# Adapter stage: the up products in two halves, VectorE's scale behind the next statistics, ScalarE's cast of z behind the gelu

## What is computed

```
h = gelu(z @ W_down[role] + b_down[role])        # 512 -> 256
u = h @ W_up[role] + b_up[role]                  # 256 -> 512
y = z + u
out = (y - mean(y)) * rsqrt(var(y) + 1e-5) * gamma[role] + beta[role]   # over the 512 features
```

## Time and profile before

| | us |
|---|---|
| median of 3 runs | 2029.14 (2028.83 to 2029.5) |
| profiled execution | 2028.81 |
| its span | 2027.2 |
| TensorE busy in the span | 2003.1 (99%) |
| VectorE busy | 1384.4 (68%) |
| ScalarE busy | 961.0 (47%) |
| GpSimd busy | 71.6 (4%) |
| adapter, from the first to the last transposes of `hs` | 116.84 |
| in it: TensorE, VectorE, ScalarE, GpSimd busy | 114.08, 107.85, 86.20, 40.94 |

### The profile page before, as it was taken

One profiled execution on the slowest core, in us unless ns is written; L12 is line 12 of the kernel. 1 busy time (PEld: TensorE's weight loads), 2 busy tenths in 40 slices (PEclk: granted clock), 3 DMA queues, 4 the chain that ended last, 5 costly groups with the idle time before them and its releaser, 6 DMA issues.

```text
span 2027.2 us, 28055 instructions
## 1 busy us (share of the span) xinstructions
PE 2003.1 (99%) x9338; PEld 1667.6 (82%) x9338; DVE 1384.4 (68%) x2567; ACT 961.0 (47%) x2009; POOL 71.6 (4%) x157
## 2 busy tenths in 40 slices
PE   8999999999999999999999999999999999999997
PEld 7888888888888878888888888888888888888886
DVE  6786785556777686555786785554787686654897
ACT  4654453433654444334564453343474454433675
POOL 0000000000000000000000000000000000000133
PEclk9999999999999999999999999999999999999999
DMA  4011232214112132124211231223202133212754
GB/s 167 32 63 42 73 104 63 63 37 151 63 52 63 53 125 63 32 63 146 73 53 42 73 99 58 63 63 120 99 32 63 43 108 115 94 58 75 258 166 126
DMA packets 106541, 169.01 MB, mean 83 GB/s; under 512 B 11168, under 2 KB 70816, under 8 KB 102688
## 3 DMA queue, kind: packets, MB, share of 16 engines
q1 hardware_dynamic: 98544, 128.81, 20.5%
q0 software_dynamic: 7776, 38.28, 5.3%
q10 hardware_dynamic: 80, 0.13, 0.0%
HBM read 136.51 MB, written 30.67 MB: 82 GB/s over the span
## 4 chain that ended last, share of the span: by engine, by line
PE 91%; DVE 4%; SPq 2%; issue 2%; DMA 1%; ACT 0%; DVEq 0%; POOL 0%; ACTq 0%; POOLq 0%
PE y L1728 16%; PE y L1730 16%; PE y L1729 16%; PE x L1728 13%; PE x L1729 13%; PE x L1730 13%; SPq L462 1%; PE y L1817 1%; PE x L1842 1%; SPq L470 1%; DVE w_lo L1155 1%; DVE c_forms L1317 0%; DVE f L1221 0%; SPq L481 0%; PE y L1816 0%
## 5 line engine op out<-in xcount | busy, mean ns | idle before, releaser
L682 ACT CAST w_hi<-w_blocks 128x512 fp32r<-128x512 f32 (+1 forms) x464 | 231.2, 519 | 122.2 <-PE y L1730 84.5
L1155 DVE TENSOR_TENSOR w_lo<-w_blocks,w_hi 128x512 fp32r<-128x512 f32 (+1 forms) x464 | 249.5, 563 | 54.7 <-ACT w_hi L682 54.7
L1728 PE MATMUL x<-h_hi,w_hi 128*128 128x512 f32 x512 | 199.7, 390 | 0.0
L1728 PE MATMUL y<-h_hi,w_hi 128*128 128x512 f32 x512 | 199.5, 390 | 0.0
L1729 PE MATMUL x<-h_lo,w_hi 128*128 128x512 f32 x512 | 199.3, 389 | 0.0
L1730 PE MATMUL x<-h_hi,w_lo 128*128 128x512 f32 x512 | 199.3, 389 | 0.0
L1729 PE MATMUL y<-h_lo,w_hi 128*128 128x512 f32 x512 | 199.3, 389 | 0.0
L1730 PE MATMUL y<-h_hi,w_lo 128*128 128x512 f32 x512 | 199.3, 389 | 0.0
L1728 PE MATMUL y<-a_forms,w_hi 128*128 128x512 f32 x480 | 187.8, 391 | 1.2 <-DVE f L1258 1.2
L1729 PE MATMUL y<-a_forms,w_hi 128*128 128x512 f32 x480 | 186.9, 389 | 0.0
L1730 PE MATMUL y<-a_forms,w_lo 128*128 128x512 f32 x480 | 186.9, 389 | 0.0
(11 more groups left out here) (235 smaller groups left out, 4194.2 us busy)
## 6 DMA issues: line engine op xcount, KB each, us to landing
w_blocks<-w1m SPq DMA_DIRECT2D x128, 256.0 KB, 3.8
w_blocks<-w1c SPq DMA_DIRECT2D x64, 256.0 KB, 3.2
w_st<-w2c SPq DMA_DIRECT2D x64, 256.0 KB, 3.2
w_st<-w2m SPq DMA_DIRECT2D x64, 256.0 KB, 4.1
zs<-z_by_batch SPq DMA_DIRECT2D x66, 128.0 KB, 2.3
cms<-f SPq DMA_DIRECT2D x32, 256.0 KB, 2.8
z_cms<-cms POOLq DMA_DIRECT2D x8, 1024.0 KB, 7.1
w_blocks<-wa_blocks SPq DMA_DIRECT2D x24, 256.0 KB, 3.7
```

The costliest lines, as they stand in the source:

```text
L682: nc.scalar.copy(w1_hi[:, w % RING, cols], src).then_inc(w1_hi_s, 1)
L1155: nc.vector.tensor_tensor(w1_lo[:, w % RING, cols], src, f32(w1_hi[:, w % RING, cols]), ALU.subtract).then_inc(w1_lo_s, 1)
L1728: nc.tensor.matmul(ps, w[0], x[0], start=first, stop=False, skip_group_check=more)
```

## The change

Three orders change, and no operation is added or taken away:

- TensorE, `up`: the four products that read `ht_hi` wait only for it, and the two that read `ht_lo` come behind them.
- VectorE, `unit`: `yo` of pair n-2 stands behind the stats of n-1 (in the old order, `yo` of n-1 ended unit n); `mv` comes before `ht_lo` of n. Behind the loop stands `yo` of pair 31, then the last pair.
- ScalarE: `split_z` is cut in two. The cast (`z_high`) of pair n+3 ends unit n. The copies (`z_biased`) stay where they were for pairs from 6 on, and stand a unit later for pairs 2 to 5; those of pair 1 come in unit 0.

```diff
-            def split_z(n, u):
+            def z_high(n, u):
 
                 if n < 2:
-                    act.wait_ge(bu_loaded, 16 * R)
                     act.wait_ge(sorted_s, 3)
                 slot = u % 4
                 act.wait_ge(zl[slot], (n - slot) * 8 + 32)
                 src = zs[:, slot].rearrange("p k c s -> p c k s")
                 nc.scalar.copy(z_hi[:, u % 2].rearrange("p c (k s) -> p c k s", k=2), src).then_inc(zh_s, 1)
+
+            def z_biased(n, u):
+
+                if n < 2:
+                    act.wait_ge(bu_loaded, 16 * R)
+                slot = u % 4
+                src = zs[:, slot].rearrange("p k c s -> p c k s")
                 r = act.value_load(role_t[0:1, bass.ds(n, 1)], min_val=0, max_val=R - 1)
                 for c in range(DC):
...
-            split_z(0, 0)
+            z_high(0, 0)
+            z_biased(0, 0)
...
-            split_z(1, 1)
+            z_high(1, 1)
...
-            def unit(n, u, z, d):
+
+            def unit(n):
                 act.wait_ge(ht_mm, n + 1)
-                nc.scalar.copy(ht_hi[:, u % 2, :], ht_ps[u % 2][:, 0:KD]).then_inc(ht_hi_s, 1)
-                if z:
-                    split_z(n + 2, u + 2)
-                if d:
-                    gelu_pair(n + 1, (u + 1) % 2)
+                nc.scalar.copy(ht_hi[:, n % 2, :], ht_ps[n % 2][:, 0:KD]).then_inc(ht_hi_s, 1)
+                if 0 < n < 5:
+                    z_biased(n + 1, n + 1)
+                if 3 < n and n + 2 < NPAIR:
+                    z_biased(n + 2, n + 2)
+                if n + 1 < NPAIR:
+                    if n == 0:
+                        z_biased(1, 1)
+                        z_high(2, 2)
+                    gelu_pair(n + 1, (n + 1) % 2)
                     if n + 3 < NPAIR:
                         down_bias(n + 3)
+                        z_high(n + 3, n + 3)
...
-            def unit(n, u, z, tail, reuse):
-
-                if tail:
+
+            def unit(n, u, z, r_old):
+
+                r = None
+                if n:
                     r = dve.value_load(role_t[0:1, bass.ds(n - 1, 1)], min_val=0, max_val=R - 1)
                     stats(n - 1, u - 1)
+                if n > 1:
+                    scale_shift(n - 2, u - 2, r_old, n - 2 >= UNROLL)
+                if n:
                     dve.wait_ge(st_s, n)
-                if n:
+                    moments(n - 1, (u - 1) % 2)
                     hidden_low(n, u)
-                if tail:
-                    moments(n - 1, (u - 1) % 2)
                     centre(n - 1, u - 1, r)
                 if z:
                     split_z(n + 2, u + 2)
-                if tail:
-                    scale_shift(n - 1, u - 1, r, reuse)
+                return r
...
             last = NPAIR - 1
+            scale_shift(last - 1, last - 1, r, True)
             r = dve.value_load(role_t[0:1, last:last + 1], min_val=0, max_val=R - 1)
             stats(last, last)
...
-                pe.wait_ge(ht_lo_s, n + 1)
+                pe.wait_ge(ht_hi_s, n + 1)
+                parts = []
                 for k in range(KD // P):
                     w = [rows(half[:, :, k, :], r) for half in (wu_hi, wu_lo)]
                     cols = slice(k * P, (k + 1) * P)
-                    ins = mm3(u_ps[u % 4][:], (ht_hi[:, u % 2, cols], ht_lo[:, u % 2, cols]), w, False,
-                              k == KD // P - 1)
+                    parts.append((w[0], cols))
+                    for half in w:
+                        nc.tensor.matmul(u_ps[u % 4][:], ht_hi[:, u % 2, cols], half, start=False, stop=False)
+                pe.wait_ge(ht_lo_s, n + 1)
+                for k, (w, cols) in enumerate(parts):
+                    ins = nc.tensor.matmul(u_ps[u % 4][:], ht_lo[:, u % 2, cols], w, start=False, stop=k == KD // P - 1)
                 ins.then_inc(u_mm, 1)
```

More of the change, by code:

```diff
@@ L1021, in gelu_pair @@
                 nc.scalar.activation(hs[:, slot, :], d_ps[slot][:, 0:KD], ACT.Gelu).then_inc(hgelu_s, 1)
-            def unit(n, u, z, d):
+            def unit(n):
                 act.wait_ge(ht_mm, n + 1)
-                nc.scalar.copy(ht_hi[:, u % 2, :], ht_ps[u % 2][:, 0:KD]).then_inc(ht_hi_s, 1)
-                if z:
-                    split_z(n + 2, u + 2)
-                if d:
-                    gelu_pair(n + 1, (u + 1) % 2)
+                nc.scalar.copy(ht_hi[:, n % 2, :], ht_ps[n % 2][:, 0:KD]).then_inc(ht_hi_s, 1)
[8 more added lines that the diff above has]
+                    gelu_pair(n + 1, (n + 1) % 2)
                     if n + 3 < NPAIR:
                         down_bias(n + 3)
+                        z_high(n + 3, n + 3)
             gelu_pair(0, 0)
             down_bias(2)
[L1035 to L1038, removed]
+            for n in range(NPAIR):
+                unit(n)
             b = act.value_load(first_t[0:1, NPAIR - 1:NPAIR], min_val=0, max_val=B - 1)
@@ L1700, in _ @@
             rest(s, 3)
+            r = None
             for n in range(NPAIR):
-                unit(n, n, n + 2 < NPAIR, n > 0, n > UNROLL)
+                r = unit(n, n, n + 2 < NPAIR, r)
                 if n < 2:
```

## The result

The changed kernel takes 2032.93 us in the median of 18 runs (2029.89 to 2034.94), the kernel before 2029.49 in 18 (2027.87 to 2033.1). The ratio is 1.0014, with a 95% interval of 1.0008 to 1.0021: about 2.9 us slower (1.6 to 4.3; the two medians are 3.4 apart). The interval leaves out 1, so this is a real loss, though under the 0.2% that the prediction took for the least change. The profiled executions are 2030.56 and 2028.81, so this one pair shows 1.75 us of it (spans 2029.0 and 2027.2).

A forecast was written before the change was run, and what follows sets the result against it. The prediction took the SP queue, which feeds z, as the bound. Head 0.4, late load 0.1 and tail 1.35 gave +1.85 on 2028.81: 2030.66 profiled, 2031.0 for the median; range 2027.2 to 2033.6.

The forecast's parts named there:

- What bounds the kernel: Whole loop: the chain of waits runs mostly through the SP queue; the loop has only 5.3 us to give.
- Part 1: TensorE up products: four run before the wait for `ht_lo`, giving it 0.9 us more room in each unit.
- part 2: VectorE order: a unit with a filler goes from 3.91 to 3.63 us; `ht_lo` stands 0.8 later behind its stats.
- Part 3: ScalarE order: z loads 6 and 7 at most 3.5 us later, all but 0.4 covered; unit 4 at most 0.5.
- the cost of a late z load: ScalarE: about 2.4 to 2.6 us from cast to next transposes, 2.49 before; 0.1 more (bounds -0.1 and 0.4).
- Where the gain goes: Loop: an early TensorE finds z not there; the SP queue's pace stays, transposes of unit 31 at 2011.0.
- The head of the SP chain (+0.4): First store: `yo` of pair 0 starts 1.28 us later, its landing shortens; 0.4 us lost (bounds 0.28 and 1.28).
- The tail (+1.35): After the loop: GpSimd's store ahead of the root delays `yo` of pair 32 from t+5.43 to t+6.78, 1.35 us lost.
- A: Rival: SP's slow steps came from collisions that the new timing avoids; 3.2 us gained, 2025.9; chance 0.10.
- C: Rival: the SP chain shortens a little, by 2 us; 2029.0; chance 0.20.
- B: Rival: SP queue gets half as many slow steps more, 4 us, before the last z load; 2035; chance 0.10.
- D: Rival: the edit does nothing to the loop, only the tail; 2030.5; chance 0.10.

The follow-up runs named there:

- sp_light_after: The changed kernel with one value load less in each unit of the SP queue, its register kept for the second-half store: 2026.24 us, ratio 0.9985 to the kernel before.
- up_vector: The kernel before with the new TensorE and VectorE orders, ScalarE as before: 2033.05 us, ratio 1.0021.
- defer_after: The changed kernel with the SP queue's stores of pairs 0 to 3 one unit later, behind one more z load each: 2029.71 us, ratio 1.0002.

## Why the prediction was right or wrong

**What bounds the kernel**: right. The chain of waits through the SP queue was no artefact; 0.42 us less in each of its units took 6.7 us from the changed kernel, and 0.42 more added 11.3.

**Part 1 and part 2**: right in kind; the number at unit 7 came out right partly by luck. VectorE's unit with a filler went to 3.66 us against a forecast of 3.63; the 0.03 is mostly that `yo` starts 0.73 behind the statistics, the upper of the two bounds. TensorE reached unit 7 2.63 us earlier, forecast 2.7, but the forecast meant the seven units, and they gave 1.73; the other 0.90 is the earlier start. VectorE's rows name waits that the forecast had at nothing: 1.03 us of `yg` of pair 0 for the load of beta (0.61 before), and twice 0.27 of `yo` for GpSimd's root. That is 0.96 more than before, which is about what is missing; no run separates these. The page "VectorE: DVE Perf Modes" of the Trainium skill, section "The DRAIN you can't avoid", measured its rule on eight equal copies and says in the same place that a next operation that is not held starts earlier. So the page by itself doesn't settle on a unit of 3.91, as the prediction read it; the trace has 0.25 us less. The claim that part 2 needs part 1's cover is right in its sign at most: 0.07 us a unit without it, in one profile.

**Part 3**: the cost of a late z load was right, 2.46 to 2.49 us from cast to transposes (2008.55 to 2011.01, 1972.17 to 1974.65), forecast 2.4 to 2.6. Not foreseen: the copies of z now stand behind a bare gap, 15 times and 6.0 us in sum ("ACT zf <- issue") against 3 and 1.2. I read it as their value load, which used to hide under the cast. It cost nothing that shows: in `sp_light_after` the gap stands 25 times, 9.3 us, beside a TensorE at its floor. Two readings were off. ScalarE is busy for 86.20 of 116.84 us, so a quarter of its unit is free and not half; unit 4 with its two sets of copies takes 3.91 us, against 3.53 in `up_vector`, which has one set there, and what of this reaches the end is not shown. And the earlier start, 0.54 us by the edit, was put at "some tenths" but stood only in a rival.

**Where the gain goes**: right. The transposes of unit 31 came at 2011.01, forecast 2011.0, behind a last load at 2005.64. That this load did not move at all is chance: the chain from the first store to it took 96.33 us against 95.87, and so gave back the 0.46 by which the first store was earlier.

**The head of the SP chain (+0.4)**: this is the step that failed. `yo` of pair 0 moved 0.84 later instead of 1.28 (1905.46 against 1904.62), because `yg` of pair 0, which waits for the load of beta in both kernels, came 0.43 earlier. Its store landed in 2.3 us instead of 3.5, so that the first store of the SP queue left 0.46 earlier, not later. But I took pair 0's store for the last one that the queue waits for. Pair 1's `yo` is later too (1909.40 against 1908.59), and the queue, now earlier, waits for its landing, 0.3 us in the first profile and 1.9 in the second. That is likely what lifts the median's difference from 1.75 to about 3 us. The page "DMA: Bandwidth & Descriptors" of the Trainium skill, section "Queues, rings and completion order", by which a store beside another queue's transfer takes turns with it, fits the sooner landing of pair 0's store; pair 1's two landings from nearly the same starts (2.4 and 3.9 us) show that the rule alone doesn't give a time.

**The tail (+1.35)**: right to 0.06. `yo` of 31 and 32 stand at t+3.66 and t+6.72, forecast t+3.72 and t+6.78; the one swap in GpSimd's queue took back 1.0 of 1.3.

**The sum**: for the profiled execution it is nearly exact, 2030.66 forecast and 2030.56 measured, and that is in part luck. It adds 0.4 for the head and 0.1 for a late load, and leaves out the 0.5 by which the prediction's own working puts the transposes of unit 31 later (2011.0 against 2010.5). Measured, the head was -0.46, its last load stood still, and the transposes moved by 0.48. So 0.5 stood in the sum for the wrong reasons; the tail was right for the right one. For the median, 2031.0 was forecast and 2032.93 measured, inside 2027.2 to 2033.6 but in its upper part; the missing 1.9 is as large as the second wait, which is likely its cause. Of the rivals, A (z is no limit) and C (a shorter SP chain) are excluded by the 13.1 us of waiting casts and by the unmoved last load, and B (4 us of slower steps in the SP queue) by that load as well. D, only the tail, is excluded by the 1.73 us that the first seven units gave.

One small misreading changes nothing: the z load behind the store of 1909.77 came 2.4 us later and not 1.9, so the mean of the twelve steps is 4.08 and not 4.12.

## What to carry to other kernels

Before costing a faster compute loop, time the queue that feeds it as a chain of its own: here value loads, DMA issues and stores of a queue that does no arithmetic took 3.5 to 3.7 us a unit, beside a TensorE at 3.48 that looked 98% busy. A gain in the loop that such a queue feeds is worth nothing until the queue is lighter, and a result that is made later can lengthen the queue's first waits, which `defer_after` shows to be worth about 3 us here. Where two engines hand work to each other in order (a store ahead of a root), look at the last two rounds by themselves: what has slack inside the loop has none at the end.

## What the runs showed that I had not expected

GpSimd's tiny addition `veps` (128x1) took 0.18 to 0.20 us in each unit of the kernel before, and up to 1.06 us in the changed one; the sums over 33 units are 6.1 and 13.7 us. In the kernel before it ran beside `yg`, which reads a PSUM bank:

```profile
1919.15 0.18 POOL L601 TENSOR_TENSOR veps<-mv,eps 128x1 f32<-128x1 f32 x1 [0.62 <-DVE mv L1652]
1919.20 0.75 DVE L1662 SCALAR_TENSOR_TENSOR yg<-x,mv,gam 128x512 f32<-128x512 f32 x1
```

In the changed kernel it falls beside `z_lo` and the filler, both with two inputs in SBUF, and ends at 1916.03, when the filler does (1915.99):

```profile
1914.71 0.68 DVE L1612 TENSOR_TENSOR z_lo<-zs,z_hi 128x512 fp32r<-128x512 f32 x1
1914.97 1.06 POOL L601 TENSOR_TENSOR veps<-mv,eps 128x1 f32<-128x1 f32 x1
1915.31 0.68 DVE L1475 TENSOR_TENSOR f<-f,z_cms 128x512 f32<-128x512 f32 x1
1915.92 0.69 DVE L1661 BATCH_NORM_STATS2 st<-x 128x6 f32<-128x512 f32 x1
```

The page "SBUF — State Buffer" of the Trainium skill, in the section "Who interferes with whom", says that a VectorE operation with both inputs in SBUF contends with GpSimd's reads; the trace agrees, at 1.06 us against 0.18. I had costed `veps` at its old duration. No run was made to separate this, so it is a reading of the timelines: in this kernel the operation beside such VectorE operations is up to nearly six times as long. The two waits of `yo` for the root inside the loop, 0.5 us in all, stand behind the two that took 1.06.

The SP queue's own steps scatter. In the chain from the first store to the last z load, with the same instructions, profiles of seven kernels lie between 94.6 and 98.3 us; value loads that take 0.27 us in the median took up to 0.96, and issues of z loads that take 0.34 took up to 1.5. This is a part of the kernel's spread from run to run, and a change of 1 us is as small as that spread.
